# Four-layer decoder on one core: last layer's loop written out, half of the keys moved ahead of the next scores, output projection and value copies moved in two kinds of slot

## The chip, the cores and the metric

The kernel runs on one core of a Trainium2 chip. The metric is the device time of one execution in microseconds (us). Below, PE is TensorE's matmul side and PEld its weight-load side, DVE is VectorE, ACT ScalarE, POOL GpSimd and SP the queue that issues most transfers. All are in-order: an instruction that waits holds up what is behind it on its engine.

## The reference, cut to what matters

The input is 32 sequences of 128 rows with 256 features, and a context of the same shape. Four attention blocks follow one another, then a routed expert network, then a fifth attention block with a gate. Each attention block has 16 heads of width 16.

```python
x = _L0(ctx, ctx, x, mask, ...)      # cross attention, layernorm, feed-forward 256->1024->256, layernorm
x = _L1(ctx, x, ...)                 # cross attention, layernorm
x = _L2(x, ctx, ...)                 # causal self attention, cross attention, then 8 experts, top 2 per row
x = _L3(x, ctx, ctx, ...)            # windowed attention (one key head), gate, rms norm, minus mean
# every attention:
scores = einsum('bqhd,bkhd->bhqk', q, k) * scale ; a = softmax(scores) ; o = einsum('bhqk,bkhd->bqhd', a, v)
x = layernorm(x + o @ wo)
```

## The kernel before, in words

The program has three stages. The first (23 to about 1252 us of the trace) does the four attention blocks and the feed-forward of the first. It is written out, no loop: 8 iterations (`ITERS`) of 16 slots, `tau` 0 to 15. In slot `tau` the block `tau // 4` (called `l` in the code, 0 to 3) does one of 4 sequences (`s`). Function `slots` calls each engine's `run` once per slot, and the order of the instructions in `run` is the order on the engine. `run` works at the same time on neighbours in the pipeline: `now` is this slot, `nxt` and `nn` are one and two slots ahead, `prev`, `ff` and `rk_` are one, two and three slots behind. Every buffer is guarded by counting semaphores.

The second stage (to about 1789 us) runs the expert network over 71 tiles. The third (to 2117 us) is the fifth block: `cslots` calls `run_c` for 32 sequences, 4 per iteration; iterations 0 and 7 are written out and iterations 1 to 6 are a hardware loop (`hinted_loop`), in which sequence numbers, and so most semaphore values, are in registers. The helper `wait_apart` adds a `sem_inc` to a wait whose value is a register.

What a slot of the first stage does on each engine, as far as the change touches it:

- PE, ordinary slot (`else` branch, slots 7 to 15 and 0 to 2): `scores(now)` (L859, masks at L826 and L833), then `project_qk(nxt)`, which is `keys` (L773; for block 0 inside `queries`, L802) and `queries` (L807, L802), a router matmul in slots 15 and 0 to 2 (L982), `av(prev)` (L924), the transpose of the maxima (L911), `xt(nn)` (L712, L727), `scores_t(now)` (L879, L886), `values(nxt)` (L785, L791), the output projection `wo(prev)` (L937), and in the slots that have block 3 two slots behind (14, 15, 0, 1: the router slots) a transpose `fxt(ff, 3)` (L712 again) into the PSUM bank of the values, so it waits for the values' copy.
- PE, feed-forward slot (3 to 6, `ff_behind`): `ff_output` (L971) comes after the scores. Behind `scores_t` come half the keys, `xt(nxt)`, the other half, then values and queries (slot 6: queries and values), then `wo`. Slots 2 to 5 end with `ff_hidden` (L958).
- ACT: `norm_apply` (L1314), `qk_evac` (L1285 to L1290), `mt_evac` (L1294), `xt_evac` (L1266 to L1272), the four `exps` of the softmax (L1301), and the copy of the values into `vz` (L1373) in all slots except 2 to 6, where DVE does it (`vz_evac`, L1527).
- DVE: `maxima(now)` (L1555), which `scores_t(now)` needs; `normalise(prev)` (L1565 to L1572, the last writes `oT` for `wo`); `qk_lo(nxt)` (L1540, L1543); `residual_sum` (L1717), which waits for `wo`; `norm_stats` (L1577 to L1582) stands ahead of the next slot's maxima.
- POOL: the roots of the norm (L2028, L2035), residual products, expansions of the queries, and in slots 7 to 10 the scatter of routed rows.

In the third stage ACT copies `wo`'s result (L1469), which DVE's `finish` (L1948) waits for; `finish` is ahead of `maxima` on DVE.

Of the kernel before, what the change touches and what calls it, by code (L numbers as in the profile page):

```python
# [15 lines left out]
P = 128  # L16
B = 32
D = 256
KC = D // P
# [7 lines left out]
NS = 4  # L27
LAYERS = 4
# [56 lines left out]
def program(nc, a, out, ctx):  # L85
# [398 lines left out]
    def cslots(run, eng):  # L484
        def iteration(j, first, last):
            for st in range(NS + (4 if last else 0)):
                run(j, st, j * NS + st, first, last)
        iteration(0, True, False)
        with hinted_loop(eng, ITERS - 1) as j:
            iteration(j, False, False)  # L490
        iteration(ITERS - 1, False, True)

    def cparts(j, st, first, last):
        def at_(d):
# [211 lines left out]
    def _(pe):  # L706
# [84 lines left out]
                    last = mm(ps_xv[:, D:2 * D], kv[:, c, :], w_attn[l][2][:, c, :], start=c == 0, stop=c == KC - 1)  # L791
            last.then_inc(v_psum, 1)

        def queries(n):
            l = n["l"]
            src = xT[n["s"]]
            wait(pe, xt_sb, n["t"] + 1)
            if l == 0:
                wait(pe, ctxt_sb, n["j"] * NS + n["s"] + 1)
                for m, (w, x_) in enumerate(((bd[0], src), (bd[1], cT[n["s"]]))):  # L800
                    for c in range(KC):
                        last = mm(ps_qk[:, D * m + P * c:D * m + P * (c + 1)], w, x_[:, c, :], start=True, stop=True)  # L802
            else:
                wq = w3q if l == 4 else w_attn[l][0]
                for o in range(KC):
                    for c in range(KC):
                        last = mm(ps_qk[:, P * o:P * (o + 1)], wq[:, c, P * o:P * (o + 1)], src[:, c, :], start=c == 0, stop=c == KC - 1)  # L807
            last.then_inc(qk_psum, 1)


        def project_qk(n, maxima):

            wait(pe, qk_lo_ready, n["t"])
            wait(pe, mt_sb, maxima)
            if n["l"] == 2:
                wait(pe, xt_sb, n["t"] + 1)
            if n["l"] != 0:
                keys(n)
            queries(n)

        def masked(blocks, strips):

# [173 lines left out]
        def run(i, tau, t, first, last):  # L996
# [29 lines left out]
            if ff_behind:  # L1026
                ff_output(rk_)
                now["ffwait"] = rk_["j"] * NS + rk_["s"] + 1
                maxima_t(now, t + 1)
                if first and tau == NS + 1:  # L1030

                    attn_loaded(2)
                    attn_loaded(3)
                    wait(pe, o_scaled, prev["t"])
                    for l, n_ in ((2, "L2_xattn_sa_bv"), (3, "L2_xattn_ca_bv")):
                        for c in range(KC):
                            last_ = mm(ps_o[:, 2 * (l - 2):2 * (l - 1), :].rearrange("p a b -> p (a b)"),
                                       col[n_][:, c:c + 1].to_broadcast([P, P]), w_attn[l][3][:, c, :], start=c == 0, stop=c == KC - 1)
                    last_.then_inc(bv_psum, 1)
                    pe.wait_ge(bv_ready, 1)  # L1040
                av(prev)
                if ranked:
                    wait(pe, ffln_step, 5 * (rk_["j"] * NS + rk_["s"]) + 1)
                    rank(ranked, ff["t"])
                if ff["l"] == 0:
                    fxt(ff, 2)
                    scores_t(now)

                    if first and nxt["s"] == 0:
                        attn_loaded(nxt["l"])  # L1050
                    wait(pe, mt_sb, nxt["t"])
                    keys(nxt, (0,))
                    xt(nxt, nxt["t"])
                    keys(nxt, (1,))
                    values(nxt, nxt["t"] + 1)
                    queries(nxt)
                    wo(prev, False, w_free)
                else:
                    scores_t(now)
                    wait(pe, mt_sb, nxt["t"])  # L1060
                    wait(pe, qk_lo_ready, nxt["t"])
                    keys(nxt, (0,))
                    xt(nxt, nxt["t"])
                    keys(nxt, (1,))
                    queries(nxt)
                    values(nxt, nxt["t"] + 1)
                    wo(prev, False, w_free)
                    xt(nn, nn["t"])
            else:
                if nxt["ok"]:  # L1070
                    if first and nxt["s"] == 0:
                        attn_loaded(nxt["l"])
                    project_qk(nxt, now["t"])
                if rk_["ok"] and rk_["l"] == 3:
                    if first and rk_["s"] == 0:
                        pe.wait_ge(ld_router, 16 * 2)
                    router(rk_, u_of(rk_), tail=not ff["ok"])
                if ranked:
                    rank(ranked, ff["t"] if ff["ok"] else NT - 1)
                if prev["ok"]:  # L1080
                    av(prev)
                if now["ok"]:
                    maxima_t_apart(now, w_free)
                if nn["ok"] and nn["l"] != 1:
                    xt(nn, nn["t"] - 1)
                if ff["ok"] and ff["l"] == 0:
                    fxt(ff, 2)
                if now["ok"]:
                    scores_t(now)
                if nxt["ok"]:  # L1090
                    if nxt["l"] == 0 and nn["l"] == 0:
                        wait(pe, ctxt_sb, nn["j"] * NS + nn["s"] + 1)
                    if ff["ok"] and ff["l"] == 0:
                        wait(pe, fxt_sb, u_of(ff) + 1)
                    values(nxt, nn["t"] + 1 if nn["ok"] and nn["l"] != 1 else nxt["t"] + 1)
                if prev["ok"]:
                    wo(prev, first and tau - 1 == 0, w_free)
                if ff["ok"] and ff["l"] == 3:
                    fxt(ff, 3 if nxt["ok"] else 0)
            if ff["ok"] and ff["l"] == 0:  # L1100
                ff_hidden(ff, u_of(ff))
        slots(run, pe)
# [149 lines left out]
    def _(act):  # L1252
# [78 lines left out]
        def run(i, tau, t, first, last):  # L1331
# [12 lines left out]
            if ff_behind:  # L1344
                mt_evac(now, mt_bank_ff)
                norm_apply(0, ff, ln_step, rstd_ready, ff["t"])
                if ff_now:
                    fxt_evac(ff, u_of(ff))
                norm_apply(1, rk_, ffln_step, ffrstd_ready, rk_["j"] * NS + rk_["s"])
                xt_evac(nxt)  # L1350
                if ff_now:
                    exps(now)
                    qk_evac(nxt)
                else:
                    qk_evac(nxt)
                    exps(now)
                    xt_evac(nn)
            else:
                if ff["ok"]:
# [8 lines left out]
                    fxt_evac(ff, u_of(ff))  # L1368
                if now["ok"]:
                    exps(now)  # L1370
                if nxt["ok"] and not ff_now:
                    wait(act, v_psum, nxt["t"] + 1)
                    nc.scalar.copy(vz[nxt["p"]][:, :, 0, :], ps_xv[:, D:2 * D].rearrange("p (h d) -> p h d", d=HD)).then_inc(vz_ready, 1)  # L1373
                if ff["ok"] and ff["l"] == 3:
# [125 lines left out]
    def _(dve):  # L1500
# [177 lines left out]
        def run(i, tau, t, first, last):  # L1678
# [88 lines left out]
            else:  # L1767
                if prev["ok"]:
                    normalise(prev)
                if nxt["ok"]:  # L1770
                    if ff["ok"] and ff["l"] == 0:
                        vz_evac(nxt)
                    if nxt["l"] == 0:
                        mask_bias(nxt)
                    qk_lo(nxt)
                if prev["ok"]:
                    residual_sum()
                router_early()
# [465 lines left out]
```

## Time and profile before

| | us |
|---|---|
| median of 3 runs (2114.21 to 2120.47) | 2120.31 |
| the profiled execution's own time | 2119.0 |
| its span, first to last instruction | 2117.2 |
| PE busy over the span | 1943.7 (92%) |
| PEld busy | 1650.0 (78%) |
| DVE busy | 1442.9 (68%) |
| ACT busy | 1213.0 (57%) |
| POOL busy | 1080.9 (51%) |
| mean granted TensorE clock | 0.979 of 2.4 GHz |

A slot of the first stage is found in the trace by its maxima on DVE (L1555): 160 of them, 128 in the first stage and 32 in the third. One steady iteration of the first stage has its slot 0 maxima at 643.3 us and the next one's at 797.15 us. A busy share is an average over the stages; what sets the length of a slot is read from the order of the engines in it, and from the idle time in brackets before an instruction, with what ended it.

### The profile page before, as it was taken

To read this page: it belongs to the slowest core of one execution; us is meant where nothing else is said; L and a number is where in the kernel's file an instruction comes from. 1 tells how busy PE (TensorE), PEld (TensorE's weight loads), DVE (VectorE), ACT (ScalarE), POOL (GpSimd) and SP (SyncE) were. 2 spreads that over 40 slices of the span, in tenths; PEclk is the share of its full clock that TensorE was granted. 3 is DMA by queue.
4 is the path that set the end of the run, shared out by engine and by line. 5 is a ranking of instruction groups with operands and counts; after the bars stand their busy time and mean duration, and the time that the engine had idled before them with its cause. 6 is when DMAs were issued, how large, how long until landed. Compare 5 with 4: busy or idle time off the path is not lost.

```text
span 2117.2 us, 70034 instructions
## 1 busy us (share of the span) xinstructions
PE 1943.7 (92%) x26048; PEld 1650.0 (78%) x26049; DVE 1442.9 (68%) x3384; ACT 1213.0 (57%) x3083; POOL 1080.9 (51%) x1592
## 2 busy tenths in 40 slices
PE   5999998998999999999999986999999997899997
PEld 4877877877877777877777765999999996677775
DVE  4577687687787786786786775444444444788886
ACT  3466466466465565565565553555555553677775
POOL 4455475475465565565564655040224002888884
PEclk9999999999999999999999996999999998899999
DMA  8501001001001001001000404121111112222220
GB/s 194 192 2 41 8 22 40 8 22 41 13 20 44 7 24 41 12 20 39 14 22 9 136 16 145 39 78 40 59 60 59 40 40 63 59 73 64 74 67 23
DMA packets 97247, 104.30 MB, mean 49 GB/s; under 512 B 23936, under 2 KB 88192, under 8 KB 96896
## 3 DMA queue, kind: packets, MB, share of 16 engines
q1 hardware_dynamic: 87936, 75.96, 11.9%
q0 software_dynamic: 8704, 25.19, 3.7%
q8 instruction: 160, 2.62, 0.5%
q14 instruction: 63, 0.52, 0.1%
q10 hardware_dynamic: 384, 0.01, 0.0%
HBM read 64.68 MB, written 36.44 MB: 48 GB/s over the span
## 4 chain that ended last, share of the span: by engine, by line
PE 73%; ACT 8%; DVE 7%; issue 5%; POOL 5%; DMA 1%; DVEq 0%; POOLq 0%; another core or an unknown queue 0%; ACTq 0%
PE ps_scores L1135 11%; PE ps_w L1148 10%; PE ps_scores L879 6%; ACT pt_all L1301 5%; PE ps_o L924 5%; PE ps_qk L807 5%; PE ps_w L971 4%; DVE mb L1555 4%; PE ps_qk L773 4%; PE ps_xv L712 3%; PE ps_w L937 3%; PE ps_qk L958 3%; PE ps_xv L958 3%; PE ps_scores L886 2%; PE ps_xv L791 2%
## 5 line engine op out<-in xcount | busy, mean ns | idle before, releaser
L1555 DVE TENSOR_REDUCE mb<-ps_scores 128x16 bf16<-128x2048 f32 x160 | 365.7, 2286 | 67.1 <-PE ps_scores L859 66.6
L1301 ACT ACTIVATE pt_all<-ps_scores 128x512 f32<-128x512 f32 x512 | 263.8, 603 | 47.3 <-PE ps_scores L886 44.3
L1399 ACT ACTIVATE tiles<-ps_scores,b1s 128x128 f32<-128x128 f32 x568 | 154.7, 384 | 202.8 <-PE ps_scores L1135 181.3
L1135 PEld LDWEIGHTS ps_scores<-tiles,w_now 128*128 128x128 f32 x2272 | 266.0, 193 | 4.8 <-issue 1.8
L1135 PE MATMUL ps_scores<-tiles,w_now 128*128 128x128 f32 x2272 | 266.5, 276 | 1.2 <-DVE tiles L1848 1.2
L2028 POOL TENSOR_TENSOR rstd<-ve,neghalf 128x1 f32<-128x1 f32 x192 | 107.2, 558 | 286.7 <-DVE ve L1581 272.3
L1148 PE MATMUL ps_w<-w_split,g_split 128*128 x1136 | 220.2, 347 | 8.0 <-DVE g_split L1867 5.5
L2005 POOL TENSOR_TENSOR qbd_all<-qT,consts 128x512 fp32r<-128x512 f32 x160 | 166.7, 1042 | 80.6 <-ACT kT L1287 72.0
L2012 POOL TENSOR_TENSOR lower<-lower,consts 128x512 fp32r<-128x512 f32 x160 | 167.0, 1044 | 72.7 <-DVE lower L1543 48.0
L1148 PEld LDWEIGHTS ps_w<-w_split,g_split 128*128 128x128 f32 x1136 | 175.5, 191 | 33.6 <-issue 9.0
L1314 ACT ACTIVATE xn<-yb,nb,rstd 128x256 f32<-128x256 f32 x160 | 95.9, 599 | 151.6 <-POOL nb L2035 148.7
L924 PE MATMUL ps_o<-pt_all,vz 128*32 128x128 f32 x5120 | 174.3, 277 | 0.8 <-DVE arena L1705 0.8
L1858 DVE TENSOR_TENSOR tiles<-ps_w,tiles 128x256 f32<-128x256 f32 x71 | 30.2, 425 | 188.1 <-PE ps_w L1148 188.1
L2118 POOL CAST w_split<-w_raw 128x256 fp32r<-128x256 f32 x64 | 23.7, 415 | 250.2 <-DVE g_split L1867 244.8
L924 PEld LDWEIGHTS ps_o<-pt_all,vz 128*32 128x32 f32 x5120 | 131.0, 110 | 23.7 <-issue 13.8
L2140 POOL DMA_INDIRECT arena<-sorted_y,pidx x64 | 63.8, 998 | 163.2 <-DMA sorted_y<-tiles 148.0
L1391 ACT COPY w_now<-w_experts 128x2048 f32 x72 | 140.1, 1947 | 9.9 <-issue 9.9
L937 PE MATMUL ps_w<-arena,oT 128*128 128x256 f32 x512 | 132.4, 381 | 2.1 <-DVE oT L1572 2.1
L1565 DVE STREAM_TRANSPOSE ps_o<-ps_o 128x512 f32<-128x512 f32 x160 | 116.4, 727 | 26.3 <-PE ps_o L924 23.6
L1272 ACT ACTIVATE xT<-ps_xv,cols_all 128x128 f32<-128x128 f32 x256 | 103.8, 457 | 51.5 <-PE ps_xv L712 48.6
L1717 DVE TENSOR_TENSOR yb<-ps_w,xr 128x256 f32<-128x256 f32 x128 | 54.2, 423 | 96.3 <-PE ps_w L937 95.5
L971 PE MATMUL ps_w<-arena 128*128 128x256 f32 x512 | 119.1, 386 | 0.0
(254 smaller groups left out, 4712.9 us busy)
## 6 DMA issues: line engine op xcount, KB each, us to landing
tiles<-sorted_x SPq DMA_DIRECT2D x72, 128.0 KB, 2.0
sorted_y<-tiles SPq DMA_DIRECT2D x71, 128.0 KB, 1.7
w_experts<-in_L_xattn_e_w SPq DMA_DIRECT2D x8, 1024.0 KB, 10.2
w_raw<-in_L_xattn_e_w POOLq DMA_DIRECT2D x8, 1024.0 KB
sorted_x<-zeros SPq DMA_DIRECT2D x8, 640.0 KB
ct_scratch<-cT SPq DMA_DIRECT2D x32, 128.0 KB, 1.8
x_scratch<-x2b_all SPq DMA_DIRECT2D x32, 128.0 KB, 1.7
arena<-x_scratch SPq DMA_DIRECT2D x32, 128.0 KB
```

Of the source, the lines that this page charges most:

```text
L879: mm(ps_s[:, g, PAIR * P * c:PAIR * P * (c + 1)], k_[at_strip, kc, :].bitcast(F32R), q_[at_strip, c].rearrange("p e q -> p (e q)").bitcast ...
L924: last = mm(ps_o[32 * q:32 * q + 32, 2 * par + c, :], vz[p][:, h].rearrange("p a d -> p (a d)"), pt[:, SLOTS * q + PAIR * c + par, :], sta ...
L937: last = mm(ps_w[:, 0:D], oT[:, c, :], w[:, c, :], start=c == 0, stop=c == KC - 1)
L971: last = mm(ps_w[:, 0:D], hT[:, j, :], w_ff2[:, j, :], start=j == 0, stop=j == FC - 1)
L1135: last = mm(ps_s[:, 2 * par + j // 4, P * (j % 4):P * (j % 4 + 1)], w1_now[:, par, c, P * j:P * (j + 1)], xgT[par][:, c, :], start=c == 0, ...
L1148: return mm(ps_w[:, 0:n], g_split[:, g_, j, :].bitcast(F32R), w2_split[:, bass.ds(odd * (2 * FC * D) + j * 2 * D, n)].bitcast(F32R), start ...
L1301: nc.scalar.activation(pt[:, 4 * g:4 * g + 4, :].rearrange("p h q -> p (h q)"), ps_s[:, g, :], ACT.Exp, bias=bias, scale=LAYER[l]["scale"] ...
L1391: nc.scalar.copy(w1_now[:, par].rearrange("p c n -> p (c n)"), w1f[:, bass.ds(e * (KC * FF), KC * FF)]).then_inc(w1_copied, 1)
L1399: last = nc.scalar.activation(gT[:, j, :], ps_s[:, 2 * par + j // 4, P * (j % 4):P * (j % 4 + 1)], ACT.Gelu, bias=b1s[par][:, j:j + 1])
L1555: V.tensor_reduce(mb[:].rearrange("p (g r) -> p g r", g=BANKS)[:, :, 0:SLOTS], ps_s[:].rearrange("p g (h k) -> p g h k", h=SLOTS), AX_X, A ...
L2005: G.tensor_tensor(qbd[p].bitcast(F32R), qT[:].unsqueeze(2).to_broadcast([P, KC, PAIR, P]), hmask.unsqueeze(1).unsqueeze(3).to_broadcast([P ...
L2012: G.tensor_tensor(qbd_lo.bitcast(F32R), qT_lo.unsqueeze(2).to_broadcast([P, KC, PAIR, P]), hmask.unsqueeze(1).unsqueeze(3).to_broadcast([P ...
```

## The change

It does five things. (1) `cslots` writes out all 8 iterations of the third stage. (2) A new function `keys_head(n)` runs half of the keys (block 0: both key products) of the slot two ahead at the end of an ordinary slot, before the next `scores`, in slots 7 to 14, and 15, 0 and 1 where they have a next slot that takes it up; `project_qk` then runs only the other half. (3) In slots 3 to 6 `wo(prev)` moves ahead of values and queries. (4) In slots 3 to 6 ACT does the first of the four `exps` ahead of `xt_evac(nxt)`. (5) In the router slots (14, 15, 0, 1) the values' copy moves from ACT, behind the exps, to DVE, behind `qk_lo`.

```diff
@@ cslots
-        iteration(0, True, False)
-        with hinted_loop(eng, ITERS - 1) as j:
-            iteration(j, False, False)
-        iteration(ITERS - 1, False, True)
+        for j in range(ITERS):
+            iteration(j, j == 0, j == ITERS - 1)
@@ tensor engine
+        def keys_head(n):
+            wait(pe, qk_lo_ready, n["t"])
+            if n["l"] == 0:
+                wait(pe, ctxt_sb, n["j"] * NS + n["s"] + 1)
+                for c in range(KC):
+                    mm(ps_qk[:, D + P * c:D + P * (c + 1)], bd[1], cT[n["s"]][:, c, :], start=True, stop=True)
+            else:
+                if n["l"] == 2:
+                    wait(pe, xt_sb, n["t"] + 1)
+                keys(n, (0,))
-        def queries(n):
+        def queries(n, keys_too=True):
-                for m, (w, x_) in enumerate(((bd[0], src), (bd[1], cT[n["s"]]))):
+                for m, (w, x_) in enumerate(((bd[0], src), (bd[1], cT[n["s"]]))[:2 if keys_too else 1]):
-        def project_qk(n, maxima):
+        def project_qk(n, maxima, headed=False):
-                keys(n)
-            queries(n)
+                keys(n, (1,) if headed else range(KC))
+            queries(n, not headed)
@@ run, feed-forward slots (both branches)
                     xt(nxt, nxt["t"])
                     keys(nxt, (1,))
+                    wo(prev, False, w_free)
                     values(nxt, nxt["t"] + 1)
                     queries(nxt)
-                    wo(prev, False, w_free)
@@ run, ordinary slots
-                    project_qk(nxt, now["t"])
+                    project_qk(nxt, now["t"], headed=tau >= 2 * NS or 0 < tau < NS - 1 or (tau == 0 and not first))
...
                     fxt(ff, 3 if nxt["ok"] else 0)
+                if nn["ok"] and (tau >= 2 * NS - 1 or tau < NS - 2):
+                    keys_head(nn)
@@ scalar engine, feed-forward slots
+                exps(now, (0,))
                 xt_evac(nxt)
...
-                    exps(now)
+                    exps(now, (1, 2, 3))
@@ scalar engine, ordinary slots: the copy into vz
-                if nxt["ok"] and not ff_now:
+                if nxt["ok"] and not (ff["ok"] and ff["l"] in (0, LAYERS - 1)):
@@ vector engine, ordinary slots
                     qk_lo(nxt)
+                    if ff["ok"] and ff["l"] == LAYERS - 1:
+                        vz_evac(nxt)
```

## Rows read from the trace of the kernel before

**Rows 1.** The page's chain of waits, shares of the span by engine.
```profile
PE 73%; ACT 8%; DVE 7%; issue 5%; POOL 5%; DMA 1%; DVEq 0%; POOLq 0%; another core or an unknown queue 0%; ACTq 0%
```
**Rows 2.** Windows: stretch, its us, busy (instructions) of PE, PEld, DVE, ACT, POOL; clock.
```profile
23.00:1252.00 1229.00, 1142.09 (x17338) 946.81 (x17337) 915.21 (x2233) 703.83 (x1777) 704.60 (x1003) 1.00 0.13 40
```
**Rows 3.** Waits: who waited for whom, us in total, times, longest.
```profile
PEld ps_xv L712 <- DVE mv L1579: 24.1, 14, 1.7
...
PEld ps_xv L791 <- ACT xT L1272: 15.4, 24, 0.6
...
PEld ps_xv L712 <- DVE st L1577: 9.5, 7, 1.4
...
PEld ps_xv L712 <- DVE yb L1717: 7.6, 8, 1.0
...
PEld ps_qk L807 <- ACT xT L1272: 6.4, 9, 1.3
```
**Rows 4.** Timeline (start, us, engine, what, idle before), end of a slot 1.
```profile
656.29 2.42 ACT L1301 ACTIVATE pt_all<-ps_scores,kmcol 128x512 f32<-128x512 f32 x4 [0.49 <-PE ps_scores L886]
...
657.81 0.42 DVE L1717 TENSOR_TENSOR yb<-ps_w,xr 128x256 f32<-128x256 f32 x1 [0.95 <-PE ps_w L937]
...
658.58 0.39 ACT L1373 COPY vz<-ps_xv 128x256 f32<-128x256 f32 x1
...
659.09 0.20 PEld L712 LDWEIGHTS ps_xv<-consts,xn 128*128 128x128 f32 x2 [1.72 <-DVE mv L1579]
...
659.46 0.10 PEld L833 LDWEIGHTS ps_scores<-x2b_all,ecol_b 32*128 32x128 bf16 x4 [0.17 <-issue]
...
660.13 2.29 DVE L1555 TENSOR_REDUCE mb<-ps_scores 128x16 bf16<-128x2048 f32 x1 [0.97 <-PE ps_scores L859]
```
**Rows 5.** Timeline, the maxima after a slot 14, no idle before it.
```profile
789.11 2.29 DVE L1555 TENSOR_REDUCE mb<-ps_scores 128x16 bf16<-128x2048 f32 x1
```
**Rows 6.** Timeline, a feed-forward slot (3).
```profile
676.05 0.60 ACT L1314 ACTIVATE xn<-yb,nb,rstd 128x256 f32<-128x256 f32 x1
...
676.54 0.45 DVE L1572 STREAM_TRANSPOSE oT<-route_all 128x256 f32<-128x256 f32 x1
...
677.00 0.53 PEld L773 LDWEIGHTS ps_qk<-cT,arena 128*128 128x128 f32 x4
...
677.31 0.81 ACT L1272 ACTIVATE xT<-ps_xv,cols_all 128x128 f32<-128x128 f32 x2 [0.66 <-PE ps_xv L712]
...
678.17 0.73 PEld L791 LDWEIGHTS ps_xv<-arena,cT 128*128 128x128 f32 x4 [0.64 <-ACT xT L1272]
...
679.92 0.73 PEld L937 LDWEIGHTS ps_w<-arena,oT 128*128 128x128 f32 x4
```
**Rows 7.** Timeline, an ordinary slot (11) from its maxima on.
```profile
759.09 2.28 DVE L1555 TENSOR_REDUCE mb<-ps_scores 128x16 bf16<-128x2048 f32 x1
...
761.13 0.62 ACT L1290 ACTIVATE kT<-ps_qk,cols_all 128x128 fp32r<-128x128 f32 x2
...
761.50 0.10 PEld L911 LDWEIGHTS ps_w<-ident_b,mb 128*128 128x128 bf16 x1 [0.20 <-DVE mb L1555]
...
761.77 0.27 ACT L1294 COPY mT<-ps_w 128x128 bf16<-128x128 bf16 x1
```
**Rows 8.** Timeline, third stage: a pause in the loop's first pass, then maxima of successive slots.
```profile
1847.02 1.57 ACT L1301 ACTIVATE pt_all<-ps_scores 128x512 f32<-128x512 f32 x3 [1.86 <-issue]
...
1942.86 2.28 DVE L1555 TENSOR_REDUCE mb<-ps_scores 128x16 bf16<-128x2048 f32 x1
...
1952.28 2.28 DVE L1555 TENSOR_REDUCE mb<-ps_scores 128x16 bf16<-128x2048 f32 x1
...
1961.62 2.28 DVE L1555 TENSOR_REDUCE mb<-ps_scores 128x16 bf16<-128x2048 f32 x1
...
2064.39 2.28 DVE L1555 TENSOR_REDUCE mb<-ps_scores 128x16 bf16<-128x2048 f32 x1
...
2073.56 2.28 DVE L1555 TENSOR_REDUCE mb<-ps_scores 128x16 bf16<-128x2048 f32 x1
```

More of the change, by code:

```diff
@@ L1064, in run @@
                     keys(nxt, (1,))
+                    wo(prev, False, w_free)
                     queries(nxt)
                     values(nxt, nxt["t"] + 1)
-                    wo(prev, False, w_free)
                     xt(nn, nn["t"])
@@ L1355, in run @@
                     qk_evac(nxt)
-                    exps(now)
+                    exps(now, (1, 2, 3))
                     xt_evac(nn)
```

## The prediction, made before the changed kernel was run

> **What bounds the kernel now.** I read the chain of waits first. Three quarters of it is PE [rows 1], so a microsecond counts only where PE itself is released earlier, or where PE is waiting. The windows say where: in the first stage, 1229 us long, PE is busy for 1142.09 [rows 2], so some 87 us of PE idle is all that reordering can give there directly. The list of waits names them. The ones that the change touches are five rows [rows 3]: 14 waits of 1.72 us, 7 of 1.36 and 8 of 0.95 in front of a transpose L712, and 24 waits of 0.64 in front of the values L791 plus eight like them in front of L807 (that row has a ninth, longer one, of another stage). Then I took the timeline of one slot of each kind. The reader has to know one trap: a releaser is the semaphore that changed last. The L712 at 659.09 is put down to DVE's norm steps, but the copy of the values on ACT (L1373) ends at 658.58 + 0.39 = 658.97, 0.12 before it [rows 4], and the copy stands behind the four exps on ACT. That copy is what L712 waits for.
>
> **Values copied by DVE (router slots).** In the slot of [rows 4] the exps end at 656.29 + 2.42 = 658.71, the copy at 658.97, the transpose starts 659.09, the scores 659.46, the maxima 660.13. With the copy on DVE, the transpose needs neither exps nor copy. DVE is idle for 0.95 ahead of `residual_sum` at 657.81, and the copy (about 0.4, as on ACT) goes into that hole, as the values are done when `wo` begins, so it costs nothing; if it did not fit it would cost 0.4 a slot. The scores then wait only for the last exp: 658.71 + 0.12 = 658.83, against 659.46, which is 0.63 earlier. Does the end of the slot follow? The maxima had 0.97 of idle before them, so DVE was free at 659.16; 660.13 - 0.63 = 659.50 is later than that, and all of 0.63 counts. Slots 0 and 1, iterations 2 to 8: 14 x 0.63 = 8.8 us. Slot 15 has the same order with shorter exps (seven waits of 1.36); I take 0.6 for it, 7 x 0.6 = 4.2. Slot 14 gives nothing: the maxima after it show no idle [rows 5], DVE was the late one. Sum 13.0. What is late next: the exps themselves.
>
> **Output projection ahead of the values, first exp ahead of the evacuation (slots 3 to 6).** These slots are PE's work end to end but for one hole. The keys' loads end at 677.00 + 0.53 = 677.53 and the values start at 678.17, 0.64 later, since xT is evacuated from 677.31 to 678.12 [rows 6]. `oT` is ready at 676.99, so `wo` can start at once; its loads take 0.73 to 0.8, so it ends at 678.3, and the values start some 0.15 later than now while the `wo` behind the queries disappears (0.75). Net 0.6. The exp in front of the evacuation: ACT's norm ends at 676.65 and then idles 0.66; an exp with the key bias is 2.42 / 4 = 0.6, so it just fits and pushes xT by nothing or by 0.05. What is new: queries end 0.15 later against the rest, so `qk_lo` on DVE is later against the second half of `ff_hidden`, which needs it. I take 0.55: 24 slots (3, 4, 5) x 0.55 = 13.2. In slot 6 the same hole is in front of the queries (the 0.64 waits at L807) [rows 3], and behind them comes a chain on ACT and DVE up to the next maxima, not PE's work. There `wo` is 0.1 to 0.2 longer than the hole and pushes the chain: 8 x -0.15 = -1.2. Bounds for the part: if the exp and `qk_lo` eat the gain, 0.1 x 24 = 2.4 and -1.6 in slot 6, so +1; if nothing is pushed, 32 x 0.64 = 20.
>
> **Half of the keys ahead of the scores.** Half the keys is 0.53 us of PE (the L773 row) [rows 6]. It goes into PE's wait for the last exp and is missing after the scores, in 87 slots. After the scores it is worth something only if PE comes late to the transpose of the maxima. In slots 15, 0, 1 and 2 it doesn't: `maxima` starts when the scores end, takes 2.29, and PE waits. In an ordinary slot [rows 7] the maxima end at 759.09 + 2.28 = 761.37 and the transpose starts at 761.50, so at most 0.13 could be had, and ACT closes even that: its evacuation of kT ends at 761.75 and mT follows at 761.77 without a pause, however early the transpose is. The start of the maxima (no idle before it) is set by `wo`, `residual_sum` and `norm_stats`, which this part doesn't move. So I count 1 us. Ends: -4 (the new semaphore wait delays the scores by 0.05 in 87 slots) and, if PE were late in all 56 ordinary slots concerned (7 x 8), 56 x 0.53 = +30.
>
> **Third stage written out.** No row shows this stage's inner iterations without a loop, but iteration 8 is already written out, and its slots can be laid beside the loop's. Maxima to maxima: 1942.86 to 1952.28 is 9.42 (with the back edge), 1952.28 to 1961.62 is 9.34, in the written-out one 2064.39 to 2073.56 is 9.17 [rows 8]. The difference is 0.17 a slot, 24 slots: 4.1 us, and 0.08 for each of some six back edges: 0.5. Part of it may come from the missing gathers of the last iteration. Against it stands new code to fetch: in the first pass of the loop ACT pauses for 1.86 us with nothing to wait for [rows 8]. That pause should go with the loop entry, or come again elsewhere. I take +4. Ends: -7 (4.1 gained, one such pause in each of six iterations, 11) and +6.5.
> The Trainium skill ("Runtime: NRT & Kernel Launch", section on instruction fetch mechanics) says that instructions are prefetched only in sequence, and that a taken branch to a page not held stalls the engine until it is fetched. By that rule alone each back edge would cost what a pause costs. The trace does not agree: its back-edge slot is only 0.08 longer than its neighbour.
>
> **Sum.** 13.0 + 13.2 - 1.2 + 1 + 4 = 30.0. From the profiled execution's own time, 2119.0: 2089.0. That execution is 1.3 below the median of the three runs shown, inside their spread of 6, so I leave the number at 2089. Clock: the first stage has it at 1.00 [rows 2] with PE 93% busy; I expect no change.
>
> **Rivals.**
> (a) The moved keys count in full, because PE, not DVE and ACT, holds the ordinary slots. For it: PEld stands still only 0.20 before the transpose [rows 7]. Against it: ACT's unbroken sequence. Time: 2089 - 29 = 2060.
> (b) The feed-forward slots give nothing, since the exp ahead of xT or the later `qk_lo` takes back what `wo` filled. For it: the exp fits into ACT's 0.66 with only some 0.05 to spare. Time: 2089 + 11 = 2100.
> (c) Writing out the third stage brings no time: the 0.17 was due to the missing gathers, and the pause moves. Time: 2093.
> (d) A taken back edge is dear, as a pause of 1.86: six of them go, 11 us in place of the 0.5. Time: 2078. Against it the 9.42. This is the skill's rule of sequential prefetch told as a mechanism of this kernel.
> (e) Slower: the written-out third stage is starved of instructions while the gathers fill the transfer engines, and ACT pauses not once per pass but in each of the 24 slots, at the place of the row of 1.86. 24 x 1.86 = 44.6, against 26.0 from the first stage, and the 4 are lost: 2119 - 26 + 44.6 = 2137.6. It decides from 26 / 24 = 1.1 us a slot. Against it: the first stage has been written out all along, with 128 slots and no such pause in the slots read.
>
> **Chances.** Forecast 0.58, (a) 0.08, (b) 0.13, (c) 0.12, (d) 0.04, (e) 0.05. The forecast's own bounds, from the ends of the parts: 2079 to 2100. The range of 8 in 10 takes in (b), (c) and (d) with some overlap, and leaves out (a) and (e): 2075 to 2106. Within 0.3% (6.4 us) of 2120 counts as no change. All cases but (e) are well below 2114; several shortfalls together could end near it. Faster 0.89, same 0.05, slower 0.06.
>
> **What would show it.** In the profile after: the waits in front of L712 by norm steps gone or under 0.3, with DVE's copy of the values counted some 30 times more; from maxima to maxima slots 15, 0 and 1 each 0.6 shorter than now, slots 3 to 5 each 0.55 shorter, slot 6 0.15 longer, and ordinary slots unchanged within 0.1, which is what rival (a) denies. Slots of the third stage at 9.17 in all iterations; a pause marked "issue" over 1 us on ACT or PE in several iterations would be (c) or (e). A gap before the second half of L958 would be (b).

## The result and the profile after

The changed kernel takes 2110.67 us (median; 2100.89 to 2122.0), the kernel before beside it 2118.86: ratio 0.9955, 95% interval 0.9942 to 0.9968. I had forecast 2089.0, with a range of 2075 to 2106. So 30 us were promised and 8 came. The profiled execution was the quickest, 2100.89.

I looked at the three stages first, as in [rows 2]. Windows of the kernel after (stretch, its us, busy and instructions of PE, PEld, DVE, ACT, POOL, clock, DMA share, GB/s), and under them one stretch cut finer:
```profile
23.00:1252.00 1229.00, 1149.95 (x17461) 971.40 (x17461) 927.72 (x2275) 698.39 (x1757) 705.67 (x1009) 0.99 0.13 40
...
253.60:257.00 3.40, 1.83 (x25) 1.07 (x24) 2.89 (x10) 2.63 (x7) 2.04 (x2) 1.00 0.00 0
257.00:260.40 3.40, 3.40 (x27) 3.14 (x29) 2.57 (x4) 1.08 (x3) 2.04 (x4) 0.50 0.00 0
260.40:277.50 17.10, 12.63 (x262) 10.49 (x254) 10.52 (x27) 9.32 (x25) 11.43 (x15) 1.00 0.10 33
277.50:280.90 3.40, 3.40 (x32) 3.02 (x24) 2.29 (x1) 0.75 (x3) 1.45 (x2) 0.50 0.00 0
```
Iterations are counted from 0 to 7 from here on. The first stage's mean clock went from 1.00 to 0.99 (a part of that is the start of the next stage, which has 1.2 GHz from 1243.5 on). The finer cut shows where: from 257.0 to 260.4 and again from 277.5 TensorE is granted 1.2 GHz, not 2.4. In the 3.40 us ahead of the first of them PE is busy for only 1.83. It is as little around the same place in iteration 2 (1.83 from 415.4 to 418.8), where the clock does not fall.

Then I listed the maxima of all 160 slots. Those that begin and end slots 7 to 11 of iteration 1, from the timeline (start, us, engine, line, what, idle before):
```profile
257.32 2.28 DVE L1568 TENSOR_REDUCE mb<-ps_scores 128x16 bf16<-128x2048 f32 x1
268.07 2.29 DVE L1568 TENSOR_REDUCE mb<-ps_scores 128x16 bf16<-128x2048 f32 x1 [1.32 <-PE ps_scores L869]
277.76 2.29 DVE L1568 TENSOR_REDUCE mb<-ps_scores 128x16 bf16<-128x2048 f32 x1 [1.36 <-PE ps_scores L869]
288.79 2.29 DVE L1568 TENSOR_REDUCE mb<-ps_scores 128x16 bf16<-128x2048 f32 x1 [1.32 <-PE ps_scores L869]
298.57 2.29 DVE L1568 TENSOR_REDUCE mb<-ps_scores 128x16 bf16<-128x2048 f32 x1 [1.52 <-PE ps_scores L869]
307.56 2.28 DVE L1568 TENSOR_REDUCE mb<-ps_scores 128x16 bf16<-128x2048 f32 x1
```
Slots 7 to 11 last 10.75, 9.69, 11.03, 9.78 and 8.99. In iterations 2 and 3 of the same execution they last 7.4, 7.8, 7.7, 7.7 and 7.7. That is 12 us lost in one iteration, and iteration 4 loses 9 in the same way (10.15, 9.60, 10.90, 9.06). I call this a series.

In a slot of a series two things are seen. Timeline, slot 7:
```profile
262.49 0.41 PE L896 MATMUL ps_scores<-mT,ecol_b 32*128 32x128 bf16 x16
...
264.66 0.61 PE L771 MATMUL ps_qk<-xT,arena 128*128 128x128 f32 x4
265.18 2.06 ACT L1313 ACTIVATE pt_all<-ps_scores 128x512 f32<-128x512 f32 x4 [2.79 <-remote]
...
267.39 0.41 PE L836 MATMUL ps_scores<-ident_b,route_all 32*128 32x128 bf16 x16 [2.12 <-ACT pt_all L1313]
```
The last matmuls of the scores are recorded as over at 262.90. The exps that need them start at 265.18, 2.28 later, and the profile finds no releaser ("remote"). PE then stands still for 2.12 ahead of the next slot. In the list of waits the exps' wait is the first row below. Seven of its nine waits are in the two series, the other two are at the start of the third stage; the kernel before has the row once, with 1.2 us, at that start.
```profile
ACT pt_all L1313 <- remote: 23.2, 9, 3.1
...
PEld ps_xv L710 <- DVE vz L1540: 11.1, 8, 1.4
...
PE ps_xv L710 <- DVE vz L1540: 7.9, 8, 1.0
```
The last two rows are new in another way: 8 waits of 0.99 each, once an iteration. They are at the end of slot 6, just where the slowed stretches begin. Timeline of it, iteration 2, slot 6:
```profile
412.93 0.73 PEld L947 LDWEIGHTS ps_w<-arena,oT 128*128 128x128 f32 x4
...
414.80 1.03 PE L789 MATMUL ps_xv<-arena,cT 128*128 128x256 f32 x4
...
416.35 0.41 DVE L1540 COPY vz<-ps_xv 128x256 f32<-128x256 f32 x1
416.82 0.20 PEld L710 LDWEIGHTS ps_xv<-consts,xn 128*128 128x128 f32 x2 [1.39 <-DVE vz L1540]
416.82 0.44 PE L710 MATMUL ps_xv<-consts,xn 128*128 128x128 f32 x2 [0.99 <-DVE vz L1540]
```
Before, the projection `wo` stood between the values and this transpose and covered DVE's copy; the PE row of the transpose had no idle (timeline of before, the same slot):
```profile
417.16 1.03 PE L937 MATMUL ps_w<-arena,oT 128*128 128x256 f32 x4
...
418.32 0.44 PE L712 MATMUL ps_xv<-consts,xn 128*128 128x128 f32 x2
```
Moved forward it leaves PE with nothing to do for 0.99.

The slots outside the series went the way that the prediction had put them. The other whole iterations last 149.6 to 150.2 against 153.8 to 154.1 before. Maxima that begin and end slots 0 and 3, and one of the third stage (timeline):
```profile
636.60 2.29 DVE L1568 TENSOR_REDUCE mb<-ps_scores 128x16 bf16<-128x2048 f32 x1
644.40 2.29 DVE L1568 TENSOR_REDUCE mb<-ps_scores 128x16 bf16<-128x2048 f32 x1 [0.37 <-PE ps_scores L869]
...
662.17 2.29 DVE L1568 TENSOR_REDUCE mb<-ps_scores 128x16 bf16<-128x2048 f32 x1 [1.23 <-PE ps_scores L869]
676.38 2.29 DVE L1568 TENSOR_REDUCE mb<-ps_scores 128x16 bf16<-128x2048 f32 x1 [1.01 <-PE ps_scores L869]
...
1835.79 2.28 DVE L1568 TENSOR_REDUCE mb<-ps_scores 128x16 bf16<-128x2048 f32 x1
1844.95 2.28 DVE L1568 TENSOR_REDUCE mb<-ps_scores 128x16 bf16<-128x2048 f32 x1
```
Slot 0 is 7.80 (before 8.40), slot 3 is 14.21 (14.90), a slot of the third stage 9.16. So the question was not which term was wrong, but what starts the series.

### The profile page after: what moved, and what is told of

The parts are those of the page before. It is cut to its first block, busy times and chain, and to the rows that moved or that the text cites. A ratio compares the mean times of both kernels' runs of the same rounds, so it can differ in the third digit from the quotient of the medians.

```text
span 2098.8 us, 68840 instructions
## 1 busy us (share of the span) xinstructions
PE 1943.5 (93%) x26048; PEld 1669.9 (80%) x26049; DVE 1445.7 (69%) x3413; ACT 1203.2 (57%) x3054; POOL 1079.9 (51%) x1592
## 4 chain that ended last, share of the span: by engine, by line
PE 65%; DVE 16%; issue 6%; POOL 5%; ACT 5%; another core or an unknown queue 1%; DMA 0%; POOLq 0%; DVEq 0%; SPq 0%
PE ps_scores L1147 12%; DVE mb L1568 10%; PE ps_w L1160 10%; PE ps_scores L889 6%; PE ps_w L947 5%; PE ps_w L981 4%; PE ps_qk L817 3%; PE ps_xv L710 3%; PE ps_xv L789 3%; ACT pt_all L1313 3%; PE ps_xv L968 3%; PE ps_qk L968 3%; PE ps_qk L771 2%; PE ps_o L934 2%; PE ps_scores L896 2%
## 5 line engine op out<-in xcount | busy, mean ns | idle before, releaser
L2055 POOL TENSOR_TENSOR xr<-xn,arena 128x256 f32<-128x256 f32 x128 | 93.2, 728 | 47.3 <-ACT xn L1326 47.3
```

## The experiments

Each kernel was timed in turns with the kernel before on its own chip. That kernel's median moved from one occasion to another (2110.5, 2114.2, 2112.0, 2124.1, 2112.6 us), so kernels are compared by their ratios. "1.2 GHz stretch" is a stretch of the records with the clock at 0.50.

### One part taken out, one part alone

**e1_no_keys_head**, the changed kernel with
```
-  project_qk(nxt, now["t"], headed=tau >= 2 * NS or ...)
+  project_qk(nxt, now["t"])
-  if nn["ok"] and (tau >= 2 * NS - 1 or tau < NS - 2):
-      keys_head(nn)
```


> The changed kernel with the keys whole again behind the scores; its other three parts stay. In the changed kernel's trace every step of the prediction is there, but in iterations 1 and 4 slots 7 to 11 are 9 to 11 us long in place of 7.4 to 7.8, with TensorE granted 1.2 GHz three and two times in them. Theory K (half of the keys ahead of the scores fills PE's pauses of the ordinary slots, and the slowed TensorE comes of that): the stretches go, and the time is that of the prediction without its 1 us, near 2090, ratio to before 0.984 to 0.988. Theory S (the 1 us pause of PE that the projection's place leaves at the end of slot 6, just ahead of the first slowed stretch, brings them): the stretches stay, 2110, ratio 0.995. Theory A (any shorter iteration brings them, by the length of the iteration against the throttle's own beat): they stay as well, 2108 to 2112.

**e2_slot6_back**, the changed kernel with, in the branch of slot 6 alone,
```
   keys(nxt, (1,))
-  wo(prev, False, w_free)
   queries(nxt)
   values(nxt, nxt["t"] + 1)
+  wo(prev, False, w_free)
   xt(nn, nn["t"])
```


> The changed kernel with the output projection of slot 6 alone behind the values again. Theory S: PE's pause at the end of slot 6 is 0.1 to 0.5 again, the slowed stretches go, near 2088, ratio 0.983 to 0.987. Theories K and A: they stay, and only the 1.1 of slot 6 comes back: 2109, ratio 0.994 to 0.996.

Measured: e1 0.9862 (0.9841 to 0.9883), e2 0.9845 (0.9828 to 0.9862). Theory K was right on e1, theory S on e2, and each was refuted by the other's run. No series was in either profile, but each has a single slowed slot. In e1, which keeps the pause of slot 6, slot 7 of iteration 1 lasts 8.85 with a 1.2 GHz stretch at its start. In e2, which has no such pause, slot 8 of iteration 7 lasts 11.73, also with a 1.2 GHz stretch; it is taken up at the end of the experiments. The flaw was in the design: I had not run the changed kernel itself beside them.

**e3_third_written_out**, the kernel before with
```
-  iteration(0, True, False)
-  with hinted_loop(eng, ITERS - 1) as j:
-      iteration(j, False, False)
-  iteration(ITERS - 1, False, True)
+  for j in range(ITERS):
+      iteration(j, j == 0, j == ITERS - 1)
```


> The kernel before with the third stage alone written out. All theories of the slowed stretches: the first stage is untouched, and the time falls by the 4 to 5 us that the third stage's slots show (9.17 in place of 9.34 to 9.42): 2113.5 to 2115.5, ratio 0.9975 to 0.998. If instruction fetch of the written-out stage costs somewhere else, 2118 or more.

Measured 0.9994 (0.9981 to 1.0007): 1.3 us, the expected 4 to 5 are just outside. `b3_before` below says why.

**e4_keys_head_only**, the kernel before with the opposite of e1's diff.

> The kernel before with half of the later keys ahead of the scores and nothing else. Theory K: slowed stretches of 10 us and more each in some iterations of the first stage, 2130 to 2140, ratio 1.005 to 1.010. Theory S: none, 2116 to 2119, ratio 0.998 to 1.000. Theory A: none or few, as the iteration is only 0.2 shorter: 2116 to 2121.

Measured 1.0056 (1.0035 to 1.0077), slower by 12 us, in the range that theory K gave, but not by its mechanism: the first stage has no series. Slots 0 and 1 last 8.84 instead of 8.40, slot 15 8.49 instead of 8.04, slot 14 8.07 instead of 7.63, in the steady iterations. Timeline of e4, slot 1:
```profile
661.82 0.41 PE L712 MATMUL ps_xv<-consts,xn 128*128 128x128 f32 x2 [1.34 <-DVE ve L1595]
...
662.06 0.64 PE L800 MATMUL ps_qk<-cT,arena 128*128 128x128 f32 x4
...
662.86 0.40 PE L871 MATMUL ps_scores<-kT,qbd_all 32*128 32x128 bf16 x16
...
663.18 0.71 PE L814 MATMUL ps_qk<-xT,arena 128*128 128x128 f32 x4
663.31 2.29 DVE L1569 TENSOR_REDUCE mb<-ps_scores 128x16 bf16<-128x2048 f32 x1 [1.45 <-PE ps_scores L871]
```
With the values still copied by ACT, L712 is late, and the moved keys (L800) stand between it and the scores that are then due.

### The changed kernel again, and the other parts alone

**a2_changed_again**: no edit.

> The changed kernel as it is, run beside the kernels without one of its parts. Without half of the keys ahead of the scores the ratio was 0.986, with slot 6's projection back behind the values 0.9845: theory K and theory S were each right by their own run, though each denied the other. Theory B (the slowed stretches need both together): this run is 0.994 to 0.997 again, with stretches of slots of 9 us and more after slot 6 in its profile, while the next kernel is at 0.984 to 0.987. Theory C (the stretches came with the chip or the moment and not with the program): this run is at 0.984 to 0.987 as well, and the profile shows no such stretch.

Measured 0.9851 (0.9829 to 0.9872). The same program that had given 0.9955 gave the ratio of the forecast (2089.0 / 2119.0 = 0.9858). There was no series, but slot 7 lasted 8.86 in iteration 2 and 8.81 in iteration 6 in place of 7.38, each with a 1.2 GHz stretch of 3.4 us at its start. The kernel is one and the same, so something of the occasion takes part in the series; chip 15 is on record for this run without a series and for run a4 below, which has one.

**e5_both_back**, the diffs of e1 and e2 together.

> The changed kernel without half of the keys ahead of the scores and with slot 6's projection behind the values: the copy by VectorE, slots 3 to 5 and the written-out third stage stay. Theory B and theory C: 0.984 to 0.987 of before. If what is left of the change brings slowed stretches too (theory A, any shorter iteration), 0.99 or more.

Measured 0.9849 (0.9826 to 0.9872). Its first stage has no 1.2 GHz stretch up to 1229.

**e6_copy_by_vectore_only**, the kernel before with
```
 (ACT)  -  if nxt["ok"] and not ff_now:
        +  if nxt["ok"] and not (ff["ok"] and ff["l"] in (0, LAYERS - 1)):
 (DVE)  +  if ff["ok"] and ff["l"] == LAYERS - 1:
        +      vz_evac(nxt)
```


> The kernel before with the router slots' values copied by VectorE and nothing else. The part is worth 14 x 0.61 and 7 x 0.62 = 12.9 us by the slots of the changed kernel: ratio 0.9935 to 0.9945. If theory A holds, it is 0.996 or more.

Measured 0.9915 (0.9897 to 0.9933), 18 us, more than expected; slots 0, 1 and 15 are 7.79, 7.79 and 7.42, as in the changed kernel, which is 12.9 by the slots. What gives the rest I have not located.

**e7_projection_and_exp_only**, the kernel before with `wo` directly behind `keys(nxt, (1,))` in slots 3 to 6 and `exps(now, (0,))` ahead of `xt_evac(nxt)`.

> The kernel before with the output projection ahead of the values in slots 3 to 6 and the first exp ahead of the evacuation, and nothing else. By the slots of the changed kernel 24 x 0.66 - 8 x 0.14 = 14.7 us: ratio 0.9925 to 0.9935. Theory S (slot 6's pause alone brings slowed stretches) : 0.997 or more, with slots of 9 us and more behind slot 6 in the profile.

Measured 0.9955 (0.9939 to 0.9971). The expected gain of the slots is there (14.2, 14.3 and 14.3 in slots 3 to 5). But slot 7, behind the pause, lasts 8.81 in each of iterations 3 to 7, and 9.90 in iteration 0 (8.39 in e8): 5 x 1.43 + 1.5 = 8.7 us given back. The time lies between the two that were expected: the clock falls behind slot 6, as theory S says, but in single stretches and not in a series. The same profile has other pauses of PE, in the router slots, where ACT still copies the values. Waits of e7:
```profile
PE ps_xv L712 <- DVE ve L1594: 18.8, 14, 1.3
...
PE ps_xv L712 <- DVE vz L1540: 8.0, 8, 1.0
```
The 14 waits of 1.3 are in slots 0 and 1, the 8 of 1.0 in slot 6. The clock fell after six of the eight. It fell after none of the fourteen, and after none of seven more of 1.0 in slot 15, so the length of one pause alone does not decide it. Since the stretches here all follow slot 6, the next test was built on this kernel.

### The pause filled

**e8_filled_pause**, e7 with, in slot 6,
```
   values(nxt, nxt["t"] + 1)
+  for _ in range(3):
+      mm(ps_o[:, 0:2, :].rearrange("p a b -> p (a b)"), oT[:, 0, :],
+         w_attn[1][2][:, 0, :], start=True, stop=True)
   xt(nn, nn["t"])
```


> The kernel with projection and first exp alone, and three more matmuls (the oT block by a weight block, 0.28 us each, into ps_o, which is read by nobody then) behind the values of slot 6, where PE otherwise waits 0.99 us for the copy. Their results are not used. In the kernel without them the slot behind slot 6 was 8.81 in place of 7.38 in iterations 3 to 7, each with TensorE granted 1.2 GHz for 3.4 us. Theory P (PE's pause at the end of slot 6 is what the clock answers to): these are gone, slot 7 is 7.38 in all of them, 5 x 1.43 = 7 us less than without the filler, ratio 0.991 to 0.993. Theory A (the length of the iteration is what counts): the iteration is as long as before the filler, and the 8.81 stay, ratio 0.995 to 0.996.

Measured 0.9919 (0.9900 to 0.9938), 7.6 us better than e7 by the ratios; the two ran on different occasions and chips; a4 and e10 below make the same comparison on one, in the changed kernel. More work on PE went with a faster kernel. Timeline and windows of e7 at the end of slot 6 of iteration 3:
```profile
565.29 0.44 PE L712 MATMUL ps_xv<-consts,xn 128*128 128x128 f32 x2 [0.99 <-DVE vz L1540]
...
567.50 2.28 DVE L1568 TENSOR_REDUCE mb<-ps_scores 128x16 bf16<-128x2048 f32 x1
576.31 2.28 DVE L1568 TENSOR_REDUCE mb<-ps_scores 128x16 bf16<-128x2048 f32 x1
```
```profile
567.30:570.70 3.40, 3.40 (x29) 3.13 (x32) 2.45 (x4) 1.33 (x4) 2.16 (x4) 0.50 0.02 5
```
and the same place in e8, where the fillers are the row of L1081 (three matmuls, each recorded twice):
```profile
561.23 1.03 PE L791 MATMUL ps_xv<-arena,cT 128*128 128x256 f32 x4
...
562.09 1.46 PE L1081 MATMUL ps_o<-arena,oT 128*128 128x256 f32 x6
...
563.39 0.38 PE L712 MATMUL ps_xv<-consts,xn 128*128 128x128 f32 x2
...
565.46 2.28 DVE L1570 TENSOR_REDUCE mb<-ps_scores 128x16 bf16<-128x2048 f32 x1
572.83 2.28 DVE L1570 TENSOR_REDUCE mb<-ps_scores 128x16 bf16<-128x2048 f32 x1
```
```profile
565.30:568.70 3.40, 3.40 (x57) 2.72 (x59) 3.22 (x5) 2.10 (x7) 2.21 (x5) 1.00 0.02 5
```
The transpose L712 has no idle ahead of it, the clock stays at 2.4 GHz, and slot 7 is 7.37 instead of 8.81. The iterations are otherwise of one length, so theory A is out.

**a3_changed_third_time**: no edit.

> The changed kernel a third time. It has given 0.9955 of before (2110.7) and 0.985 of before (2084.5). Theory C (what came between is a disturbance of single executions or of one chip, not of the program): 0.984 to 0.987 again where the profile shows no series of stretched slots behind slot 6, and 0.994 to 0.997 where it does. If it lies between, near 0.990, the series come and go on one chip.

Measured 0.9859 (0.9833 to 0.9884). Slot 7 lasts 8.80 in iterations 2, 4 and 7 and 9.90 in iteration 0; no series.

**b3_before**: the kernel before, profiled on that occasion.

> The kernel before, profiled beside the others. The kernels of the other runs that keep the loop of the third stage have 36.8 us for an iteration of it from iteration 3 on, the profile of before that the prediction used has 37.4. If the chip or the moment makes the difference: 36.8 here, and writing the stage out is worth under 1 us as in its own experiment. If the rest of those kernels does: 37.4 here.

Maxima of its third stage, one iteration apart:
```profile
1949.05 2.28 DVE L1555 TENSOR_REDUCE mb<-ps_scores 128x16 bf16<-128x2048 f32 x1
...
1985.84 2.28 DVE L1555 TENSOR_REDUCE mb<-ps_scores 128x16 bf16<-128x2048 f32 x1
```
36.79 an iteration with the loop. The loop slots of [rows 8] last 9.42 and 9.34, and such an iteration 37.4. A written-out iteration takes 36.68 (9.17 a slot). Writing it out is worth 0.1 an iteration here.

**e9_copy_and_keys_head**, the diffs of e6 and e4 together.

> The kernel before with two parts: the values of router slots copied by VectorE, and half of the later keys ahead of the scores. Alone the copy gave 0.9915 and the keys 1.0056. Theory of the late transpose (alone, the keys stand between the late transpose L712 and the scores and push those by 0.44 in slots 15, 0 and 1; with the copy on VectorE the transpose is early and they fit into the wait for the last exp): slots 15, 0, 1 are 7.42, 7.79, 7.79, the ratio is 0.990 to 0.9925. If the keys cost the same in any company: 0.9915 x 1.0056 = 0.997.

Measured 0.9926 (0.9904 to 0.9947), slots 15, 0, 1 at 7.42, 7.79, 7.78: with the copy on DVE the moved keys cost nothing there. The keys do not repeat their price of 12 us in this company; they bring no measurable gain either (0.9926 against 0.9915).

### The pause filled, moved away and doubled in the changed kernel

The next four ran on one occasion, on which the kernel before took 2124.1.

**a4_changed_fourth_time**: no edit.

> The changed kernel a fourth time, as the one that the next three are laid beside. Without series of stretched slots 0.984 to 0.987; where they come again as in its first profile (slots 7 to 11 of an iteration at 9 to 11 us), 0.990 to 0.997.

**f2_slot6_back_again**: e2 again.

> The changed kernel with slot 6's projection behind the values, again, now beside the changed kernel itself. Theory P (PE's pause of 0.99 at the end of slot 6 is what TensorE's clock answers to, and the series of the first profile starts from it): 0.982 to 0.986 whatever the changed kernel does in these rounds, 2 to 6 us below it where that has only single slowed stretches, and 20 to 30 below it where it has series. Theory C alone (series come with the moment, the pause has no part in them): both move together, within 3 us.

**e10_changed_filled_pause**: e8's filler in the changed kernel.

> The changed kernel with the three unused matmuls in slot 6's pause. Theory P: no slot of 8.8 behind slot 6 in any iteration, and 0.982 to 0.985, 2 to 6 us below the changed kernel; slot 6 itself stays at 13.34. Against it: some 8.8 slots stay, and the time is the changed kernel's.

**e11_longer_pause**, the changed kernel with, in slot 6 on DVE,
```
   qk_lo(nxt)
+  wait(dve, v_psum, nxt["t"] + 1)
+  V.tensor_reduce(spare[:], ps_xv[:, D:2 * D].unsqueeze(1).to_broadcast([P, 4, D]), AX_X, ALU.max)
   vz_evac(nxt)
```


> The changed kernel with one more read of the values by VectorE (128x1024 in all, about 1.15 us by the maxima's 2.28 for 128x2048) ahead of the copy in slot 6: PE's pause there is 2.1 in place of 0.99. Its result is not used. Slot 6 gets 1.15 longer, 8 x 1.15 = 9.2 us, 0.0044. If that is all: 0.989 to 0.991. Theory P: more iterations than the two or three of now have a slot 7 of 8.8 or more, and if the pause also feeds the series, slots 8 to 11 are stretched as well: 0.993 to 1.000.

| kernel | PE's pause in slot 6 | us (median, range) | ratio (95%) |
|---|---|---|---|
| a4, changed | 0.99 | 2108.0 (2088.0 to 2112.1) | 0.9924 (0.9901 to 0.9946) |
| f2, `wo` back | none | 2089.1 (2086.8 to 2091.8) | 0.9833 (0.9810 to 0.9856) |
| e10, filled | none | 2080.9 (2077.3 to 2086.8) | 0.9800 (0.9775 to 0.9824) |
| e11, longer | 2.12 | 2137.2 (2126.5 to 2152.9) | 1.0056 (1.0033 to 1.0080) |

This time the series were there: one of a4's seven executions took 2088.0, the other six 2103.7 to 2112.1. Even the 2088.0, the profiled one, has a series, in iteration 2 (10.17, 9.59, 10.92, 9.04). Both ways of removing the pause remove all slowed slots 7 in iterations 1 to 7, and theory C alone (both move together) is refuted. Doubling it put series into iterations 1, 3, 5 and 7. Waits of e11, its windows, and its timeline in iteration 3:
```profile
ACT pt_all L1314 <- remote: 46.2, 17, 3.0
...
PE ps_scores L837 <- ACT pt_all L1314: 35.8, 20, 2.2
...
PE ps_xv L711 <- DVE vz L1541: 17.0, 8, 2.1
```
```profile
579.10:582.50 3.40, 3.40 (x24) 3.16 (x26) 2.19 (x1) 0.85 (x2) 2.18 (x4) 0.50 0.02 5
...
599.60:603.00 3.40, 3.40 (x40) 3.03 (x28) 2.29 (x1) 0.60 (x1) 1.45 (x2) 0.50 0.02 5
```
```profile
579.01 2.28 DVE L1569 TENSOR_REDUCE mb<-ps_scores 128x16 bf16<-128x2048 f32 x1
590.36 2.29 DVE L1569 TENSOR_REDUCE mb<-ps_scores 128x16 bf16<-128x2048 f32 x1 [1.32 <-PE ps_scores L870]
600.30 2.29 DVE L1569 TENSOR_REDUCE mb<-ps_scores 128x16 bf16<-128x2048 f32 x1 [1.65 <-PE ps_scores L870]
```
The "remote" row went from 5 times in a4's profile (3 of them in its series) to 17 (16 in series). The pause itself costs little: slot 6 is 13.94 instead of 13.34, 8 x 0.6 = 4.8 us, out of 29 between a4 and e11.

f2 is not free of slowed slots. It has no pause in slot 6, but in iteration 7 its slots 8 to 10 last 11.51, 9.20 and 10.58, a short series. Timeline and windows of f2 there:
```profile
1170.51 0.40 PE L896 MATMUL ps_scores<-mT,ecol_b 32*128 32x128 bf16 x14 [2.14 <-issue]
```
```profile
1171.70:1175.10 3.40, 3.40 (x30) 2.73 (x32) 1.12 (x5) 1.53 (x4) 1.75 (x2) 0.50 0.09 27
```
Here too PE stood still just before the clock fell, for 2.14 us in which it waited for nothing that the profile shows ("issue"). PE has the same pause in slot 8 of iteration 7 in seven other profiles, all with the moved keys. In e4, e2 and a2 it lasts 1.80 to 2.31, and the clock falls in it or within 1.2 us behind it; in a3 it lasts 2.06, and in the changed kernel's first profile, in a4 and in f3 1.30 to 1.52, and the clock does not fall. No experiment moved or filled this pause.

**f3_longer_pause_again**: e11 again, on another occasion.

> The kernel with the longer pause in slot 6 again, as control for the next: it gave 1.0056, with slots 7 to 11 stretched in iterations 1, 3, 5 and 7. If the series come with that pause wherever it runs: 0.998 to 1.008 and such series again. If they need a chip or a moment as well: between 0.989 and 0.995 with single slowed slots.

**e13_longer_pause_no_keys_head**: e11 with e1's diff.

> The same without half of the keys ahead of the scores. If the pause alone makes the series: slots 7 to 11 stretched as in the control, within 0.003 of its ratio. If the moved keys are the other half of it (they fill PE's 0.28 to 0.53 ahead of the scores, and the stretched slots all have their signals of scores_t 2.2 us late, in the slots with moved keys): single slots 7 of 8.8 to 9 at most, and 0.989 to 0.995.

Measured f3 0.9911 (0.9898 to 0.9925), e13 0.9945 (0.9926 to 0.9964), both profiles without a series. Slot 7 is 8.9 or longer in three iterations of f3 and in five of e13. The control failed to bring series, so whether the moved keys are needed for one stays open.

## Why the prediction was wrong

**The step that failed** is the sentence on the clock: "the first stage has it at 1.00 [rows 2] with PE 93% busy; I expect no change." It read a mean over 1229 us as a property of the kernel, and so put the clock at nothing in the sum. The runs showed in its place that the change opened a pause of 0.99 us of PE at the end of slot 6, and that the clock falls to 1.2 GHz behind it. On the one occasion on which all were run together, the changed kernel was at 0.9924, with the pause filled at 0.9800, with the pause moved away at 0.9833 and with it doubled at 1.0056. What turns a single slowed stretch into a series stays open. In the profiled execution the two series cost 12.0 and 9.2 us; 2100.9 less 21 is 2080. The other executions of the first timing were up to 21 us longer at mean clocks of 0.972 to 0.975, against 0.976. They have no trace; that this too is series is inferred.

**Slot 6** was seen and priced as "0.1 to 0.2 longer than the hole", on the chain to the next maxima. That was right (13.34 against 13.20). What I did not ask is what `wo` had covered where it stood: DVE's copy of the values, in front of the next transpose. Moving it by two places made a PE wait of 0.99 that costs the slot nothing by itself, and 8.8 or 10 us slots behind it.

**Values by DVE:** forecast 13.0; slots as forecast (0.61 and 0.62), alone 18. Right, if anything small. **Slots 3 to 5:** forecast 0.55 a slot, measured 0.65 to 0.69; e8, where nothing is given back, has 17.1 us for the part, forecast 12.0. Rival (b) is out. **Keys:** forecast 1; nothing measurable in e9 over e6 or in the changed kernel over e1, so rival (a) is out. Beside the longer pause they are worth more: f3 is 7 us faster than e13, and the two intervals do not overlap. They give 0.13 to 0.2 in each of slots 9 to 11, and something goes back in iteration 7: slot 8 lasts 9.3 to 12.6 there in nine of the eleven profiles with them and 7.8 to 7.9 in all without, against 1.1 gained in slot 9. In eight of the nine this is the pause of 1.3 to 2.3 us shown under f2; the ninth, e11, has a series there. But "in slots 15, 0, 1 and 2 it doesn't [matter]" held only because the copy moved too; alone the keys cost 12 us. **Third stage:** forecast 4, measured 1.3 with up to 4 inside its interval. Most of the 0.17 a slot of [rows 8] belonged to that profiled execution and not to the loop, so rival (c) is nearer, for a reason it did not give. Rivals (d) and (e) are out: no series of pauses came in the third stage, where all slots from iteration 2 on are 9.17.

**The sum**, 30.0 from 2119, is a ratio of 0.9858. Runs a2 and a3, with single slowed stretches, gave 0.9851 and 0.9859. So the sum came out where the series stayed away and was 22 us too good where they did not. That it came out so closely was in part luck: slots 3 to 5 gave 24 x 0.67 = 16.0 us for 13.2, the third stage 1.3 for 4, and every single slowed slot took 1.4. The range should have held the second case. I gave it no chance because no rival was about PE's own clock. Even without it, with the low ends of its own parts, 13.0 + 1 - 4 - 7 = 3, the range would have reached 2116 and not 2106.

**The better version** came out of this: the changed kernel without the pause. e10 (0.9800) and f2 (0.9833) beat both kernels on the occasion with series, and their executions lie within 10 us where a4's scatter over 24. Which of the two is better their intervals leave open. Against the changed kernel without series (0.9851 and 0.9859) e2 gained nothing clear (0.9845).

## What to carry to other kernels

When work is moved forward on the engine that sets the time, look at what it covered in its old place, and do so even where the slot's length does not depend on it. A pause of 1 us in TensorE in otherwise dense work can cost more than itself. If the clock's records show dips, look for a pause just ahead of them, and fill it with unused matmuls as a test: it takes two lines and asks the question directly. Run the unchanged candidate beside its ablations on the same chip and the same occasion; e1 and e2 alone had supported two theories that each denied the other.

## What the runs showed of the hardware

- A pause of 0.99 us of PE was followed by a 3.4 us stretch at 1.2 GHz in some iterations and not in others of the same length (four of eight in a3, none behind slot 6 with the pause filled in e10). Pauses of 1.35 in the router slots of the kernel before, 14 of them, were followed by none. What picks them I don't know. The Trainium skill ("TensorE: Matmul & The Clock Gate", section "A second HAM failure mode: psum-queue depth-cycling") tells of a kernel in which short idle times of PE between groups of matmuls made its clock go back and forth. These traces agree that short idle times are enough, and differ in how often they come: there frequently, here one such pause in an iteration of 150 us.
- With three useless matmuls in the pause the changed kernel's ratio to before fell from 0.9924 to 0.9800 on one occasion (a4, e10), and that of the part alone from 0.9955 to 0.9919 on two (e7, e8).
- In a series the completion signals of the scores' last matmuls come 1.7 to 2.4 us after their modelled ends, in slots at the 2.4 GHz level as well: 12.63 us of PE in 17.10 between the two slowed stretches. Single 1.2 GHz stretches cost slot 7 1.4 us (1.2 to 1.6 beside the longer pause of f3 and e13) and have no such lag. A lag of 1.6 also stands at the start of the third stage in e10, whose first stage has no series. Its cause is open: no experiment isolates it.
- The same kernel before took 2110.5 to 2124.1 us from one occasion to another, and the changed kernel, or e11, had series on two of the five on which one of them ran. It is not the chip alone: chip 15 is on record for a2, without a series, and for a4, with one.
